# First chunks of W2 and W3 loaded as two transfers of 256 columns each

## The reference

```python
def L0_cond(x, w, ids):        # a 512 x 512 matrix per batch, chosen by id
    return einsum('bsi,boi->bso', x, w[ids])
def L0_ffn(x, W1, b, A, B, starts):   # W1 x + b + low-rank adapter by segment
    ...
def L1_cond(x, W2, b2, a, b, scale, ids):
    return einsum('bsi,oi->bso', x, W2) + b2 + scale * (x @ a.T @ b.T)
def L1_ffn(x, W3, b3, A, Bmat, LiMEs):
    H = einsum('btd,od->bto', x, W3) + b3
    ...                        # a router over 8 experts, from a few columns
    return H + delta
x = x + L0_ffn(L0_cond(x, W0, ids0), ...)
x = x + L1_ffn(L1_cond(x, W2, ..., ids1), W3, ...)
```

## Time and profile before

| | |
|---|---|
| median of 3 runs | 122.10 us (121.98 to 122.14) |
| profiled execution, its own time | 122.28 us |
| its span in the trace | 120.3 us |
| PE busy | 115.6 us (96%) |
| DVE busy | 84.1 us (70%) |
| ACT busy | 58.5 us (49%) |
| POOL busy | 23.5 us (20%) |
| read from memory, written | 16.39 MB, 2.10 MB |

### The profile page before, as it was taken

How to read it: one execution, slowest core, us unless ns; L and a number is a source line. 1 busy time by engine, 2 the same in 40 slices (tenths; PEclk the granted TensorE clock), 3 DMA queues, 4 the chain that set the end, 5 groups by cost and what they waited for, 6 DMA issues and landing times.

```text
span 120.3 us, 1976 instructions
## 1 busy us (share of the span) xinstructions
PE 115.6 (96%) x694; PEld 98.5 (82%) x694; DVE 84.1 (70%) x176; ACT 58.5 (49%) x102; POOL 23.5 (20%) x49
## 2 busy tenths in 40 slices
PE   6899999999999999999999999999999999999991
PEld 2488878888989897998989998799988588688890
DVE  0499978896688979868897424859967676404831
ACT  4289388985978485888356343140650110230000
POOL 3038000049000999900014000000000000000000
PEclk9999999999999999999999999999999999999999
DMA  3999999829999889999194000000000000000972
GB/s 86 405 421 328 406 415 398 349 78 249 253 330 368 268 218 306 253 269 244 35 339 182 0 0 0 5 0 0 0 0 0 5 0 0 0 0 3 347 264 86
DMA packets 7353, 20.78 MB, mean 173 GB/s; under 512 B 1200, under 2 KB 1584, under 8 KB 7344
## 3 DMA queue, kind: packets, MB, share of 16 engines
q1 hardware_dynamic: 5424, 16.03, 39.1%
q0 software_dynamic: 1632, 4.28, 11.7%
q10 hardware_dynamic: 288, 0.36, 0.8%
HBM read 16.39 MB, written 2.10 MB: 154 GB/s over the span
## 4 chain that ended last, share of the span: by engine, by line
PE 87%; DVE 4%; DMA 3%; ACT 3%; issue 1%; ACTq 0%
PE bank L879 70%; DMA w_in<-in_W 3%; PE bank L999 3%; PE bank L1002 3%; PE bank L996 2%; PE bank L916 2%; PE bank L1078 1%; PE bank L990 1%; ACT a L431 1%; DVE w_lo L715 1%; ACT w_hi L402 1%; DVE x_in L612 1%; PE bank L978 1%; PE bank L1149 1%; PE bank L1068 1%
## 5 line engine op out<-in xcount | busy, mean ns | idle before, releaser
L559 DVE TENSOR_TENSOR w_lo<-w_in,w_hi 128x1024 fp32r<-128x1024 f32 x16 | 19.2, 1221 | 3.0 <-ACT w_hi L396 3.0
L879 PE MATMUL bank<-c_hi,w_hi 128*128 128x256 f32 x64 | 18.2, 284 | 0.0
L879 PE MATMUL bank<-c_hi,w_lo 128*128 128x256 f32 x64 | 18.1, 283 | 0.0
L879 PE MATMUL bank<-c_lo,w_hi 128*128 128x256 f32 x64 | 18.1, 283 | 0.0
L396 ACT CAST w_hi<-w_in 128x1024 fp32r<-128x1024 f32 x16 | 16.3, 1050 | 2.2 <-DMA w_in<-in_W 2.2
L879 PE MATMUL bank<-m_hi,x_hi 128*128 128x512 f32 (+1 forms) x36 | 13.9, 387 | 0.0
L879 PE MATMUL bank<-m_hi,x_lo 128*128 128x512 f32 (+1 forms) x36 | 13.3, 368 | 0.0
L879 PE MATMUL bank<-m_lo,x_hi 128*128 128x512 f32 (+1 forms) x36 | 13.2, 367 | 0.0
L879 PE MATMUL bank<-w_hi,x_hi 128*128 128x512 f32 x32 | 13.2, 412 | 0.0
L879 PE MATMUL bank<-w_hi,x_lo 128*128 128x512 f32 x32 | 12.6, 393 | 0.0
L879 PE MATMUL bank<-w_lo,x_hi 128*128 128x512 f32 x32 | 12.5, 391 | 0.0
(11 more groups left out here) (184 smaller groups left out, 243.4 us busy)
## 6 DMA issues: line engine op xcount, KB each, us to landing
w_in<-in_W SPq DMA_DIRECT2D x21, 512.0 KB, 7.3
out_dram<-w_in SPq DMA_DIRECT2D x7, 256.0 KB, 2.2
be<-late_t POOLq DMA_DIRECT2D x16, 69.0 KB, 7.5
x_in<-in_x SPq DMA_DIRECT2D x2, 512.0 KB, 7.5
b<-low_t POOLq DMA_DIRECT2D x16, 64.0 KB, 5.5
x_in<-in_x POOLq DMA_DIRECT2D x2, 512.0 KB, 8.9
w_in<-in_W SPq DMA_DIRECT2D x1, 1024.0 KB, 6.0
late_t<-in_late SPq DMA_DIRECT2D x1, 552.0 KB, 3.5
```

Source lines behind the costliest of these rows:

```text
L559: nc.vector.tensor_tensor(part(w_lo[:, b % 2], h), raw(b, h), f32(part(w_hi[:, b % 2], h)), ALU.subtract).then_inc(w_lo_done, 1)
L879: ins = mm(o, st, mv, start=start and n == 0, stop=stop and n == len(parts) - 1)
```

## The change

The load of chunk 0 is cut into halves of 256 columns. SP issues W3's columns 0 to 255 and then 256 to 511 with a semaphore each (`w3_0_landed[0]` and `[1]`), in front of chunk 1. ACT does the same with W2 (`w2_0_landed[0]` and `[1]`), in front of `early_t`. The cast of each half waits for its own half alone: ACT has a wait in front of each of its two casts of W3, DVE one in front of each of its two casts of W2. `w23_landed` keeps entries for chunks 1 to 3 only. Casts, matmuls, their order and what they wait for among the engines stay as they are.

```diff
-        w23_landed = [sem(f"w23_landed{c}") for c in range(C)]
-        w2_0_landed = sem("w2_0_landed")
+        w23_landed = [None] + [sem(f"w23_landed{c}") for c in range(1, C)]
+        w2_0_landed, w3_0_landed = ([sem(f"{w}_0_landed{h}") for h in range(2)] for w in ("w2", "w3"))
...
-            sp.dma_start(w_in[:, 0, D:2 * D], W23[0][:, D:2 * D]).then_inc(w23_landed[0], 16)
+            for h in range(2):
+                at = slice(D + D // 2 * h, D + D // 2 * (h + 1))
+                sp.dma_start(w_in[:, 0, at], W23[0][:, at]).then_inc(w3_0_landed[h], 16)
             load_w23(1)
...
-            act.dma_start(w_in[:, 0, 0:D], W23[0][:, 0:D]).then_inc(w2_0_landed, 16)
+            for h in range(2):
+                act.dma_start(w_in[:, 0, half_of(h)], W23[0][:, half_of(h)]).then_inc(w2_0_landed[h], 16)
             act.dma_start(early_t[:], early).then_inc(early_landed, 16)
-            act.wait_ge(w23_landed[0], 16)
             for h in range(2):
+                act.wait_ge(w3_0_landed[h], 16)
                 nc.scalar.copy(w1_hi[:, 0, half_of(h)], w23_in(0, 1)[:, half_of(h)]).then_inc(w3_hi0_done, 1)
...
                 if c == 0:
-                    dve.wait_ge(w2_0_landed, 16)
                     for h in range(2):
+                        dve.wait_ge(w2_0_landed[h], 16)
                         nc.vector.tensor_copy(w_hi[:, 1, 0, half_of(h)],
                                               w23_in(0, 0)[:, half_of(h)]).then_inc(w2_hi0_done, 1)
```

## The result

The changed kernel takes 124.27 us (median of 4, 123.87 to 124.36) where the kernel before takes 122.08 (121.98 to 122.14): slower by 2.2 us. The comparison's own ratio, which isn't the plain quotient of the medians, is 1.0152 [1.0112, 1.0192]. The profiled execution took 124.36 us with a span of 122.4. The forecast was 122.0.

The account below looks back on a forecast made before the run. TensorE bounds the kernel (busy 115.6 of 120.3 us); the change works only on its 0.36 us wait for the W2 cast. L999 starting 0.09 us earlier gave 122.10 - 0.09 = 122.0 us, range 121.7 to 122.35.

Parts of the forecast that it names:

- First halves: First 256 columns of chunk 0's W2: complete at about 3.2 us, used by the cast at 3.8 to 3.9.
- The first two matmuls: First two of PE's half product (L990 before, L993 after): start at 4.46 us, through before 5.0, hidden in idle 0.36.
- The second half, d = 0.25: How much later W2's second half lands than whole W2 did: 0.13 us for packets plus 0.12 for sharing.
- the sharing argument: W2's remaining packets take turns with chunk 1's 4 KB packets on the DMA engines: 0 to +0.14 us.
- The clock rises at 5.9: PE goes from 1.2 to 2.4 GHz at about 5.9 us; matmuls brought before it cost 0.21 instead of 0.12.
- L1002 of chunk 0 at 6.35: Chunk 0's product after the half product (L999 before the change) starts at 6.35 us, 0.09 earlier.
- What else moves: Loads behind the halves: SP's five big loads +0.13 us; early_t, issued 0.4 later, lands about 6.3, still covered.
- Cover: Slack before PE would wait: 0.5 us behind DVE's early_t work in chunk 1, 0.66 at m_lo of bank 0.
- One for one to the end: Later stages follow PE, so what is won or lost at L999 (L1002 after) reaches the end in full.
- (1): W2's second half, caught between chunk 1's packets, becomes PE's wait: d = 1.6, 1.0 us lost, 123.1; chance 0.09.
- (4): Halves of chunk 0's loads land together, so the split does nothing: 122.1 to 122.3 us; chance 0.1.
- signs of being wrong: Second cast starting past 5.0 us, 0.21 us matmul spacing ending elsewhere than 5.9, or a new wait on PE.

Follow-up runs that it names:

- experiments 7 and 9: 7: kernel before, chunk 1 and early_t held by DVE memset: 0.9996, 1.0129, 1.0041. 9: DVE's row numbers behind chunk 1: kernel before 0.9968, with late issue 1.0045.
- experiment 8: Changed kernel with DVE's row numbers moved behind chunk 1: 1.0048; beside it the changed kernel unedited: 1.0081; both against the kernel before.
- experiment 1: One queue split at a time: only W3, made in the changed kernel, 1.0118; only W2, made in the kernel before, 1.0145.

## Why the prediction was wrong

- **First halves** used at 3.8 to 3.9: measured 3.52 and 3.66. Right in kind. The bytes came a little sooner: by 3.0 us the ACT queue has moved 0.12 MB, where the earlier trace rows have 0.10.
- **The first two matmuls** in the warm matmuls' shadow: right, PE passes from L1009 to L993 without a wait.
- **The second half, d = 0.25 in a range of 0 to 0.67**: measured 4.38, d = -0.20, outside the range. In the two later profiles with the same loads it was 4.81 and 5.06, d = 0.23 and 0.48. The three go with chunk 1's first cast, 8.53, 7.51 and 6.59: the later chunk 1's packets come, the less they disturb W2. That fits the sharing argument. But the reference point scatters too: whole, W2 was used at 4.58 before and between 4.20 and 4.53 in five other unsplit profiles (experiments 7 and 9), so one trace couldn't give d to 0.1.
- **The clock rises at 5.9**: not in this execution. L1002's matmuls still start 0.43 apart at 6.17, 6.60 and 7.03 (1.2 GHz) and 0.23 apart from 7.29 on, so it rose at about 7.1, with PE having run without a gap since 1.07. It put off L1005 by 0.4 (7.52 is 1.35 behind L1002's start; before, 7.37 is 0.93 behind 6.44) and cost nothing at the end, as PE idled before 9.72 anyway. In experiment 8's profiles of the same start L993's last matmuls come 0.12 apart from 5.39 and from 5.63 on, so there it had risen by then. The Trainium skill ("TensorE: Matmul & The Clock Gate", Part 1) says that the same kernel can catch it at another moment in another run; the runs agree with that sentence, which the prediction set aside on three close timings.
- **L1002 of chunk 0 at 6.35**: 6.17, and 5.99 and 6.23 in the two others. That is 0.2 to 0.45 us before the 6.44 of one trace. But in the six unsplit profiles in which W2 was used by 4.6 the same place lies between 5.92 and 6.78, so how much of it is the split's and how much the clock's isn't shown.
- **The failed step** stands in "What else moves": "they move by bytes and packets: +0.13", and `early_t` "lies queued behind W2 anyway and shifts with d: about 6.3, still covered". Measured: chunk 1 +2.60 (8.53 for 5.93) and `early_t` about 8.7. Both sentences took a transfer's landing for a matter of bytes ahead of it, so that an issue 0.47 later into a full queue is free. The queue wasn't full then: the engines' share fell to 0.28. The trace of before could hardly show otherwise: SP's third transfer, chunk 2, was issued 0.9 behind the first there too, but had chunk 1's 512 KB ahead of it, and ACT had no third. The error was to give the move of the issue no bound of its own, though the two transfers moved were the ones that PE needs next; chunk 1's own cover was not worked out at all.
- **Cover**: the argument for DVE's row numbers (8.67 against 9.18, 0.5 us) had the right mechanism, and a delay of 2.5 goes far through it. Of the 0.66 at `m_lo` 0.29 was left in the changed kernel (there at 20.88, read at 21.17), and none in experiment 1.
- **One for one to the end**: right, +2.13 at L1005 of chunk 1 and +2.1 of span.
- **Rivals**: (1) came true in the run with W2 alone split: matmul 3 at 6.61 for 6.6, the next product at 7.57 for 7.4, and behind it the fall of the clock, which it hadn't priced. (4) is out, as the halves were used 0.7 apart. The case that decided, what stands behind the halves landing late, was not among them. Two of the prediction's signs of being wrong did appear: the 1.2 GHz spacing ended elsewhere, and PE had waits that the earlier trace rows don't have.

## What to carry to other kernels

Cutting a first load in two cost little here by its bytes. It cost by what stands behind it in its queue: each further issue puts that off by 0.4 to 0.5 us, and in most profiles with 0.76 us or more between a queue's first issue and this one the landing came 1 to 2 us later still. Why is open, so measure it rather than sum bytes. Before putting an issue ahead of others at a kernel's start, list who waits for the ones moved and give their delay a bound far above the shift in issue time. A step that needs a small early table is best put behind work that doesn't, where nobody waits for its result: that alone gave 0.3% here, just clear of noise. And when a run is slower than another, look at which wait PE has and at its clock before charging the difference to the edit.

## What the runs showed of the hardware

- A 512 KB transfer issued 0.76 to 1.25 us after the first of its queue took 4.2 to 6.8 us to land, where it was 4.3 to 4.8 for one issued 0.44 to 0.65 after, and 3.3 for one issued to idle engines. In the two slowest of them the 16 engines' share was 0.28 to 0.83 from 3.6 to 6 us. It strikes some executions and spares others.
- W3 and W2, issued together on two queues, landed 0.17 to 0.19 us apart in all nine profiles in which both were whole (used at 4.39 and 4.58 before).
- In the run with 64-row transfers their issues took 0.57 to 0.87 us, and 0.59 and 0.61 those of 128 rows right behind; elsewhere 128 rows took 0.34 to 0.47.
- POOL took 0.91 us to issue two half blocks as one transfer, which landed 6.4 us after its issue's start; SP's halves landed after 2.6 to 2.9.
- The first rise of TensorE's clock, seen by the spacing of matmuls, came at about 3.8 (W2 alone split), 5.4 (experiment 8), 5.9 (before) and 7.1 (after), in executions that all start with the same eight warm-up matmuls at 1.07. The granted-clock column reads 1.00 before that rise too.
